# Attention inside an AdaLN block: value operands packed into one stationary tile, row sums of the exponentials on GpSimd, O kept for 1024 queries

## The chip, the cores and the metric

One core of one Trainium2 chip runs the whole program. The metric is the device time in microseconds. Five engines work beside each other, each through its own instructions in order, and wait for each other on semaphores: TensorE (PE), VectorE (DVE), ScalarE (ACT), GpSimd (POOL) and SyncE (SP, which only issues transfers here).

## The reference

All tensors are float32; x is 2 x 2048 x 256.

```
mod = (silu(c) @ wmod).reshape(2, 6, 1, 256)         # sa, ca, ga, sb, cb, gb
h = layernorm(x) * (1 + ca) + sa
x = x + ga * token_statistics_attention(h)           # the front of the kernel
h = layernorm(x) * (1 + cb) + sb
x = x + gb * ffn(h)

def ffn(X):                                          # 4 heads of 64
    nx = rmsnorm(X, g1)
    Q  = (nx @ Wq.T) in 4 heads;  Kc = nx @ Wkc.T;  Vc = nx @ Wvc.T     # K and V shared by the heads
    scores = einsum("bhsd,btd->bhst", Q, Kc) / 8
    X = X + (softmax(scores) @ Vc, heads side by side) @ Wo.T
    ... router over 8 experts, top 2, swiglu experts plus a shared one
```

## The kernel before

The program has three stages. The **front** (to about 233 us of the profile) makes the first residual and the first K, V and Q. The **loop** (about 235 to 1113 us) is the softmax attention of the second half. The **tail** runs 110 expert tiles and combines them.

The loop has 256 steps, numbered gs. A step belongs to one pair of batch and head, bh = gs // 32 (bh 0 to 3 are batch 0). In a bh, steps 0 to 15 take the first 1024 queries (qc = 0) and steps 16 to 31 the second 1024 (qc = 1), each against one block kc of 128 keys. Float32 products are made from fp32r parts: a high part, and a low part that is the value less its high part. One step is:

- `qk(gs)` on PE, 4 matmuls of 512 columns: scores, keys on the partitions, into banks 0 and 1, or 2 and 3.
- `exp(gs)` on ACT: `PT` = exp of the scores (L770), then `PH`, its rounded high part (L775). PT has 2 buffers, PH and PL have 3.
- `low(gs)`: `PL` = PT - PH (L1189 on DVE; every fourth step, up to step 243, L1514 on POOL, by `by_pool`). PT, PH and PL all lie in SBUF.
- `av(gs, n)` on PE, for each half n of 512 queries, 3 matmuls: VH x PH, VL x PH, VH x PL (L1749 to L1751), summed over the 16 key blocks in banks 4 and 5. VH carries a 65th column of ones and VL one of zeros, so that row 64 of the result is the sum of the exponentials.
- after the 16th key block, `o_out` copies 65 x 512 to `O` on ACT; `O` holds all 2048 queries of a bh.

PE runs, for each gs: `qk(gs + 1)`, jobs, `av(gs - 1, 0)`, jobs, `av(gs - 1, 1)`, jobs. DVE runs `low(gs)` and then the jobs of the step. The jobs are spread over the steps by `loop_order`, at positions 0 to 96 of a bh, three to a step. They are: `max_mm` (one matmul of 512 columns on PE, then a maximum over it on DVE, L1159; 64 for each bh, for the softmax shift), `proj` (O times Wo on PE, L1713, then DVE takes the reciprocal of column 256, L1176, and adds to X2, L1180; 16 for each bh, run during the next bh), and in some bh the making of the next Q (`q_mm`, `q_hi`: two ACT copies and two POOL copies of 64x512, L1507; `q_lo`: two DVE subtractions of 64x512, L1153), of K and V of batch 1 (`nx_scale`, `k_mm`, `v_mm`), the router (`rl_scale`, `choose`, `place`) and `scatter`. Every job with a result in PSUM takes bank 6 or 7 in turn (`Banks`): PE waits until the job two before has been read.

The wait of `exp` on the step two before stands in three lines:

```
            if gs >= 2:
                low_done(w, gs - 2)
            act.activation(PT[:, gs % 2, :], PS[:, bk:bk + 2, :].rearrange("p a n -> p (a n)"), ACT.Exp,
```

`after_last` makes each POOL instruction wait for the POOL instruction before it. The tail begins with 16 `proj` of bh 7, nine jobs a tile.

## Time and profile before

| | |
|---|---|
| median of 3 runs | 1458.81 us (1456.15 to 1462.72) |
| the profiled execution | 1461.01 us |
| its span, first to last instruction | 1459.0 us |
| mean granted TensorE clock | 0.967 of full speed |
| the loop in it | about 240 to 1113 us |
| busy over the span | PE 1307.4, DVE 1079.0, ACT 893.1, POOL 385.4 us |

A busy time is the union of an engine's instructions; those of PE overlap each other in the record, so that PE's share overstates its work: a matmul of 512 columns is recorded with some 395 ns and the next one starts 0.23 us after it. An instruction that is held up after its start is recorded longer, not as idle.

### The profile page before, as it was taken

To read this page: it belongs to the slowest core of one execution; us is meant where nothing else is said; L and a number is where in the kernel's file an instruction comes from. 1 tells how busy PE (TensorE), PEld (TensorE's weight loads), DVE (VectorE), ACT (ScalarE), POOL (GpSimd) and SP (SyncE) were. 2 spreads that over 40 slices of the span, in tenths; PEclk is the share of its full clock that TensorE was granted. 3 is DMA by queue.
4 is the path that set the end of the run, shared out by engine and by line. 5 is a ranking of instruction groups with operands and counts; after the bars stand their busy time and mean duration, and the time that the engine had idled before them with its cause. 6 is when DMAs were issued, how large, how long until landed. Compare 5 with 4: busy or idle time off the path is not lost.

```text
span 1459.0 us, 19334 instructions
## 1 busy us (share of the span) xinstructions
PE 1307.4 (90%) x6008; PEld 920.7 (63%) x6008; DVE 1079.0 (74%) x2143; ACT 893.1 (61%) x1450; POOL 385.4 (26%) x282
## 2 busy tenths in 40 slices
...
GB/s 196 1 1 44 15 58 208 81 1 1 1 1 1 1 1 1 1 1 1 1 1 1 1 1 44 1 0 1 22 51 65 104 93 117 195 148 165 191 115 149
DMA packets 56418, 75.82 MB, mean 52 GB/s; under 512 B 8383, under 2 KB 48063, under 8 KB 56064
## 3 DMA queue, kind: packets, MB, share of 16 engines
...
## 4 chain that ended last, share of the span: by engine, by line
PE 63%; DVE 19%; issue 5%; ACT 5%; POOL 5%; DMA 1%; ACTq 1%; POOLq 0%; DVEq 0%; SPq 0%
PE PS L1802 8%; PE PS L1700 6%; PE PS L1749 6%; PE PS L1732 6%; PE PS L1751 6%; PE PS L1735 6%; PE PS L1750 6%; DVE mx L1159 5%; PE PS L1828 4%; DVE PL L1189 4%; PE PS L1713 3%; POOL y L1534 2%; PE PS L1686 2%; POOL xbuf L1522 2%; PE PS L1786 1%
## 5 line engine op out<-in xcount | busy, mean ns | idle before, releaser
L1159 DVE TENSOR_REDUCE mx<-PS 128x1 f32<-128x512 f32 x512 | 344.1, 686 | 100.6 <-PE PS L1700 98.5
L770 ACT ACTIVATE PT<-PS 128x1024 f32<-128x1024 f32 x256 | 262.8, 1027 | 231.8 <-PE PS L1735 221.8
L1514 POOL TENSOR_TENSOR PL<-PT,PH 128x1024 fp32r<-128x1024 f32 x61 | 146.2, 2396 | 541.8 <-ACT PH L775 530.1
L775 ACT ACTIVATE PH<-PT 128x1024 fp32r<-128x1024 f32 x256 | 271.2, 1060 | 8.1
L1189 DVE TENSOR_TENSOR PL<-PT,PH 128x1024 fp32r<-128x1024 f32 x195 | 238.9, 1225 | 44.4 <-ACT PH L775 43.8
L1749 PE MATMUL PS<-PH,VH 128*65 128x512 f32 x512 | 219.6, 429 | 8.6 <-DVE PL L1189 8.6
L1751 PE MATMUL PS<-PL,VH 128*65 128x512 f32 x512 | 202.9, 396 | 0.0
L1750 PE MATMUL PS<-PH,VL 128*65 128x512 f32 x512 | 202.3, 395 | 0.0
L1700 PE MATMUL PS<-KA,Q 128*128 128x512 f32 x384 | 161.1, 432 | 16.9 <-DVE mx L1159 12.1
L1732 PE MATMUL PS<-Q,KA 128*128 128x512 f32 x384 | 128.0, 415 | 2.5 <-POOL KB L1491 2.5
L1735 PE MATMUL PS<-Q,KB 65*128 65x512 f32 x384 | 122.6, 401 | 0.0
L1700 PEld LDWEIGHTS PS<-KA,Q 128*128 128x128 f32 x384 | 73.5, 192 | 65.7 <-DVE mx L1159 35.4
L1751 PEld LDWEIGHTS PS<-PL,VH 128*65 128x65 f32 x512 | 69.7, 136 | 49.6 <-issue 1.0
L1750 PEld LDWEIGHTS PS<-PH,VL 128*65 128x65 f32 x512 | 70.2, 137 | 47.9 <-issue 4.6
L1522 POOL DMA_INDIRECT xbuf<-nxT,slot x64 | 64.0, 1000 | 134.7 <-DVE nxT L1347 117.4
L1749 PEld LDWEIGHTS PS<-PH,VH 128*65 128x65 f32 x512 | 70.2, 137 | 41.3 <-issue 13.6
L1713 PE MATMUL PS<-woa,O 65*128 65x257 f32 x256 | 80.8, 402 | 12.0 <-DVE mx L1159 8.6
L1534 POOL DMA_INDIRECT y<-ybuf,slot x64 | 62.1, 970 | 107.8 <-DVE X L1401 71.2
L1369 DVE TENSOR_TENSOR xl<-PS,xh 128x256 fp32r<-128x256 f32 x110 | 46.3, 421 | 56.4 <-ACT xh L857 56.1
L1735 PEld LDWEIGHTS PS<-Q,KB 65*128 65x128 f32 x384 | 73.7, 192 | 17.5
L1732 PEld LDWEIGHTS PS<-Q,KA 128*128 128x128 f32 x384 | 71.9, 191 | 19.9 <-issue 3.4
L864 ACT ACTIVATE sg<-PS 128x256 f32<-128x256 f32 x110 | 42.4, 385 | 59.9 <-PE PS L1802 59.7
...
## 6 DMA issues: line engine op xcount, KB each, us to landing
...
```

Source lines behind the costliest of these rows:

```text
L770: act.activation(PT[:, gs % 2, :], PS[:, bk:bk + 2, :].rearrange("p a n -> p (a n)"), ACT.Exp, scale=0.125).then_inc(sem("pt"), 1)
L775: act.activation(PH[:, gs % 3, :], PT[:, gs % 2, :], ACT.Copy).then_inc(sem("pt_h"), 1)
L1159: dve.tensor_reduce(mx[:, half, i, c:c + 1], PS[:, k, :], AX, ALU.max).then_inc(sem("dve_out"), 1)
L1189: dve.tensor_tensor(PL[:, gs % 3, :], PT[:, gs % 2, :], phf[:, gs % 3, :], ALU.subtract).then_inc(sem("pl_v"), 1)
L1514: pool.tensor_tensor(PL[:, gs % 3, :], PT[:, gs % 2, :], phf[:, gs % 3, :], ALU.subtract).then_inc(sem("pl_g"), 1)
L1700: pe.matmul(PS[:, k, :], QA[bh % 3][:, q0:q0 + P], KA[b][:, c * 512:c * 512 + 512], start=True, stop=True).then_inc(sem("pe_use"), 1)
L1713: pe.matmul(PS[:, k, 0:257], O[0:65, i * P:i * P + P], woa[0:65, bh % 4, :], start=True, stop=True).then_inc(sem("pe_use"), 1)
L1732: pe.matmul(PS[:, bk + n, :], KA[b][:, kc * P:kc * P + P], QA[qs][:, q0:q0 + 512], start=True, stop=False)
L1735: mm = pe.matmul(PS[:, bk + n, :], KB[b][0:65, kc * P:kc * P + P], QB[qs][0:65, q0:q0 + 512], start=False, stop=True)
L1749: pe.matmul(PS[0:65, 4 + n, :], VH[:, t, :], PH[:, r, c], start=(kc == 0), stop=False)
L1750: pe.matmul(PS[0:65, 4 + n, :], VL[:, t, :], PH[:, r, c], start=False, stop=False)
L1751: pe.matmul(PS[0:65, 4 + n, :], VH[:, t, :], PL[:, r, c], start=False, stop=(kc == 15)).then_inc(sem("av"), 1)
```

## The change

Four things. (1) VH and VL become one tile `V` of 128 columns, 64 high and 64 low: PH is multiplied once by all 128 columns, PL by the 64 high ones, 4 value matmuls a step in place of 6. Rows 64 to 127 of the result hold the part of VL; `proj` multiplies all 128 rows of O by Wo, written twice one under the other. (2) The ones column is gone. POOL keeps a running sum over the key blocks, `Z`, one 128x1024 instruction for each step (`total`: a copy for kc = 0, else Z = Z + PT), and `z_mm` multiplies Z by a column of ones on PE, once for every 1024 queries: 8 plain float32 matmuls of one column; DVE takes one reciprocal for 8 proj. (3) All 256 `low` are on DVE, PL has 2 buffers in place of 3, and `exp(gs)` waits for `low(gs - 2)` and `total(gs - 2)`. (4) O holds 1024 queries. `proj` of the first 1024 queries runs in the same bh (positions 53 to 92), those of the second in the next (5 to 46), so the tail keeps 8 `proj` and not 16.

```diff
-POOL_EVERY = 4
@@ loop_order
+        todo += [(50, ("z_mm", bh, 0))] + spread(proj_jobs(bh, 0), 53, 92)
         if bh > 0:
-            m, e = (30, 60) if bh == 4 else (49, 92)
-            todo += spread(proj_jobs(bh - 1)[:8], 4, m) + spread(proj_jobs(bh - 1)[8:], m + 1, e)
+            todo += [(3, ("z_mm", bh - 1, 1))] + spread(proj_jobs(bh - 1, 1), 5, 46)
@@ tail_order
-    last = [x for j, p in enumerate(proj_jobs(7)) for x in (p, norm[j])] + [norm[NT]]
+    last = [("z_mm", 7, 1)] + [x for j, p in enumerate(proj_jobs(7, 1)) for x in (norm[j], p)] + norm[8:]
@@ tiles
-    VH = sb("VH", [P, NB * NT, 65], F32R, c=c3)
-    VL = sb("VL", [P, NB * NT, 65], F32R, c=c3)
+    V = sb("V", [P, NB * NT, 2, 64], F32R, c=c3)
-    PL = sb("PL", [P, 3, 1024], F32R, c=c3)
-    O = sb("O", [65, S], c=c3)
-    woa = sb("woa", [65, 4, 257], c=c3)
+    PL = sb("PL", [P, 2, 1024], F32R, c=c3)
+    Z = sb("Z", [P, 2, 1024], c=c3)
+    O = sb("O", [P, 1024], c=c3)
+    woa = sb("woa", [P, 4, D], c=c3)
@@ ACT, exp
             if gs >= 2:
-                low_done(w, gs - 2)
+                w.wait_ge(sem("pl"), gs - 1)
+                w.wait_ge(sem("z"), gs - 1)
@@ DVE
+        def z_mm(bh, qc):
+            ...
+            dve.reciprocal(rz[:, qc, :], PS[:, k, 0:8]).then_inc(sem("dve_out"), 1)
@@ DVE, proj
-            mark(dve.reciprocal(rz[:, s, :], PS[:, k, 256:257]))
@@ DVE, low
-            if gs >= 3:
-                w.wait_ge(sem("av"), 2 * (gs - 2))
-            dve.tensor_tensor(PL[:, gs % 3, :], PT[:, gs % 2, :], phf[:, gs % 3, :], ALU.subtract).then_inc(sem("pl_v"), 1)
+            if gs >= 2:
+                w.wait_ge(sem("av"), 2 * (gs - 1))
+            dve.tensor_tensor(PL[:, gs % 2, :], PT[:, gs % 2, :], phf[:, gs % 3, :], ALU.subtract).then_inc(sem("pl"), 1)
@@ DVE loop
-            if not by_pool(gs):
-                low(gs)
+            low(gs)
@@ POOL
+        def total(gs):
+
+            g, kc = divmod(gs, 16)
+            w.wait_ge(sem("pt"), gs + 1)
+            if kc == 0:
+                ...
+                pool.tensor_copy(Z[:, g % 2, :], PT[:, gs % 2, :]).then_inc(sem("z"), 1)
+            else:
+                after_last("z")
+                pool.tensor_tensor(Z[:, g % 2, :], Z[:, g % 2, :], PT[:, gs % 2, :], ALU.add).then_inc(sem("z"), 1)
@@ POOL loop
-            if by_pool(gs):
-                low(gs)
+            total(gs)
@@ PE
+        def z_mm(bh, qc):
+            w.wait_ge(sem("ones"), 1)
+            w.wait_ge(sem("z"), 16 * (2 * bh + qc + 1))
+            k = bank("z_mm", bh, qc, 0)
+            for i in range(8):
+                mm = pe.matmul(PS[:, k, i:i + 1], Z[:, qc, i * P:i * P + P], ones[:, :], start=True, stop=True)
+            mm.then_inc(sem("pe_use"), 1)
@@ PE, av
-            pe.matmul(PS[0:65, 4 + n, :], VH[:, t, :], PH[:, r, c], start=(kc == 0), stop=False)
-            pe.matmul(PS[0:65, 4 + n, :], VL[:, t, :], PH[:, r, c], start=False, stop=False)
-            pe.matmul(PS[0:65, 4 + n, :], VH[:, t, :], PL[:, r, c], start=False, stop=(kc == 15)).then_inc(sem("av"), 1)
+            if kc < 15:
+                pe.matmul(PS[:, 4 + n, :], V[:, t, :, :].rearrange("p a d -> p (a d)"), PH[:, gs % 3, c], start=(kc == 0),
+                          stop=False)
+                pe.matmul(PS[0:64, 4 + n, :], V[:, t, 0, :], PL[:, gs % 2, c], start=False, stop=False).then_inc(sem("av"), 1)
+            else:
+                ...
```

What the change does to the order of POOL's instructions is seen from the last step of bh 0 on. Before, POOL stands there with the copies of `q_hi` (L1507) and one low part (L1514) for every fourth step; a number behind x counts repeated instructions.

```order
58 L1514 TENSOR_TENSOR PL<-PT,PH 128x1024
59 L1507 COPY Q<-Q 64x512
60 L1507 COPY QA<-QA 64x512
61 L1514 TENSOR_TENSOR PL<-PT,PH 128x1024 x13
```

After the change the same copies (now L1499) stand between the running sums (L1514) of every step; L1511 is the copy that begins a new sum.

```order
67 L1514 TENSOR_TENSOR Z<-Z,PT 128x1024 x4
68 L1499 COPY Q<-Q 64x512
69 L1499 COPY QA<-QA 64x512
70 L1514 TENSOR_TENSOR Z<-Z,PT 128x1024 x3
71 L1499 COPY Q<-Q 64x512
72 L1499 COPY QA<-QA 64x512
73 L1514 TENSOR_TENSOR Z<-Z,PT 128x1024 x4
74 L1511 COPY Z<-PT 128x1024
75 L1514 TENSOR_TENSOR Z<-Z,PT 128x1024 x15
```

POOL went from one 128x1024 instruction in four steps to one in each. The second place is the end of bh 7, where `scatter` issues its indirect transfers from POOL's queue. Before, the last low part of POOL lies ahead of all of them.

```order
69 L1514 TENSOR_TENSOR PL<-PT,PH 128x1024 x18
70 L1522 DMA xbuf<-nxT,slot 4992x256 x64
71 L1534 DMA y<-ybuf,slot 128x256 x40
```

After the change they alternate with the running sums, two or four transfers to a sum.

```order
103 L1514 TENSOR_TENSOR Z<-Z,PT 128x1024
104 L1522 DMA xbuf<-nxT,slot 4992x256 x4
105 L1514 TENSOR_TENSOR Z<-Z,PT 128x1024
106 L1522 DMA xbuf<-nxT,slot 4992x256 x2
107 L1514 TENSOR_TENSOR Z<-Z,PT 128x1024
108 L1522 DMA xbuf<-nxT,slot 4992x256 x4
```

Thirty-two of the transfers now have sums between them, and `exp` waits for these sums. The third place is DVE's stream in the middle of the loop. Before, steps whose low part is POOL's have no L1189, so that DVE's jobs of two steps follow each other.

```order
643 L1189 TENSOR_TENSOR PL<-PT,PH 128x1024
644 L1159 TENSOR_REDUCE mx<-PS 128x1 x2
645 L1176 RECIPROCAL rz<-PS 128x1
646 L1180 SCALAR_TENSOR_TENSOR X2<-PS,rz,X2 128x256
647 L1159 TENSOR_REDUCE mx<-PS 128x1 x2
648 L1176 RECIPROCAL rz<-PS 128x1
649 L1180 SCALAR_TENSOR_TENSOR X2<-PS,rz,X2 128x256
650 L1159 TENSOR_REDUCE mx<-PS 128x1
651 L1189 TENSOR_TENSOR PL<-PT,PH 128x1024
```

After, a low part (L1182) stands in every step, with two or three maxima (L1146) and at times a proj (L1173) behind it.

```order
659 L1182 TENSOR_TENSOR PL<-PT,PH 128x1024
660 L1146 TENSOR_REDUCE mx<-PS 128x1 x2
661 L1182 TENSOR_TENSOR PL<-PT,PH 128x1024
662 L1146 TENSOR_REDUCE mx<-PS 128x1 x3
663 L1182 TENSOR_TENSOR PL<-PT,PH 128x1024
664 L1146 TENSOR_REDUCE mx<-PS 128x1 x2
665 L1182 TENSOR_TENSOR PL<-PT,PH 128x1024
666 L1146 TENSOR_REDUCE mx<-PS 128x1
667 L1164 RECIPROCAL rz<-PS 128x8
```

The step-wise alternation of a low part and its jobs is now the same in all steps, and the reciprocal stands once for eight proj.

## Rows read from the trace of the kernel before

**Rows 1.** The page: busy time of each engine over the span.
```profile
PE 1307.4 (90%) x6008; PEld 920.7 (63%) x6008; DVE 1079.0 (74%) x2143; ACT 893.1 (61%) x1450; POOL 385.4 (26%) x282
```

**Rows 2.** Windows, the loop by bh: us, then busy us (instructions) per engine, clock.
```profile
240.00:331.00 91.00, 90.40 (x385) 61.56 (x384) 72.63 (x96) 67.18 (x67) 19.19 (x8) 1.00 0.27 91
...
558.00:678.00 120.00, 115.45 (x503) 78.26 (x501) 89.10 (x137) 77.19 (x85) 26.56 (x16) 0.99 0.00 1
...
1010.00:1113.00 103.00, 90.93 (x384) 60.04 (x383) 77.59 (x153) 66.72 (x70) 42.20 (x34) 0.98 0.13 44
sum 873.00, PE 834.36 PEld 557.81 DVE 667.73 ACT 590.55 POOL 202.41; mean PE 104.29 PEld 69.73 DVE 83.47 ACT 73.82 POOL 25.30
```

**Rows 3.** The page: costliest groups, busy us, mean ns, idle before and releaser.
```profile
L1159 DVE TENSOR_REDUCE mx<-PS 128x1 f32<-128x512 f32 x512 | 344.1, 686 | 100.6 <-PE PS L1700 98.5
L770 ACT ACTIVATE PT<-PS 128x1024 f32<-128x1024 f32 x256 | 262.8, 1027 | 231.8 <-PE PS L1735 221.8
L775 ACT ACTIVATE PH<-PT 128x1024 fp32r<-128x1024 f32 x256 | 271.2, 1060 | 8.1
```

**Rows 4.** Timeline, 602 to 605 us, PE and PEld: start, us, instruction.
```profile
602.38 0.40 PE L1751 MATMUL PS<-PL,VH 128*65 128x512 f32 x1
602.38 0.19 PEld L1700 LDWEIGHTS PS<-KA,Q 128*128 128x128 f32 x1
602.61 0.39 PE L1700 MATMUL PS<-KA,Q 128*128 128x512 f32 x1
```

**Rows 5.** One line's instructions, L1514 and L1189: ns min/median/max.
```profile
L1514 POOL TENSOR_TENSOR PL<-PT,PH x61: 2340/2393/2499, 245.2 to 1069.8; 128x1024 fp32r<-128x1024 f32 x61
...
L1189 DVE TENSOR_TENSOR PL<-PT,PH x195: 1210/1217/1503, 237.3 to 1111.1; 128x1024 fp32r<-128x1024 f32 x195
```

**Rows 6.** Timeline, 336 to 344 us: DVE and POOL about a `q_hi` and `q_lo`.
```profile
336.05 0.61 POOL L1507 CAST QA<-QA 64x512 fp32r<-64x512 f32 x1 [9.62 <-ACT QA L761]
...
336.30 1.44 DVE L1189 TENSOR_TENSOR PL<-PT,PH 128x1024 fp32r<-128x1024 f32 x1
...
336.81 1.40 POOL L1507 CAST Q<-Q 64x512 fp32r<-64x512 f32 x1 [0.16 <-POOL QA L1507]
...
339.52 2.50 POOL L1514 TENSOR_TENSOR PL<-PT,PH 128x1024 fp32r<-128x1024 f32 x1 [1.31 <-ACT PH L775]
...
339.80 2.77 DVE L1153 TENSOR_TENSOR Q<-qst,Q 64x512 fp32r<-64x512 f32 x1
```

**Rows 7.** One line's instructions, L1153, L1507 and L1159: ns min/median/max.
```profile
L1153 DVE TENSOR_TENSOR Q<-qst,Q x24: 671/687/2769, 201.0 to 833.3; 64x512 fp32r<-64x512 f32 x24
...
L1507 POOL CAST Q<-Q x24: 604/612/1457, 201.1 to 831.3; 64x512 fp32r<-64x512 f32 x24
...
L1159 DVE TENSOR_REDUCE mx<-PS x512: 627/690/694, 203.1 to 1051.2; 128x1 f32<-128x512 f32 x171
```

**Rows 8.** Groups by form: proj, its reciprocal, `nx_scale` and PE's small float32 matmuls.
```profile
L1180 DVE SCALAR_TENSOR_TENSOR X<-PS,rz,X 128x256 f32<-128x256 f32 x128 | 61.9, 484 | 4.5
...
L1176 DVE RECIPROCAL rz<-PS 128x1 f32<-128x1 f32 x128 | 20.7, 162 | 26.7 <-PE PS L1713 26.3
...
L1133 DVE TENSOR_SCALAR nx<-X,rs 128x256 f32<-128x256 f32 x32 | 17.2, 541 | 0.1
```

**Rows 9.** Timeline, 385 to 389 us: an `nx_scale` beside a low part on POOL.
```profile
385.53 2.41 POOL L1514 TENSOR_TENSOR PL<-PT,PH 128x1024 fp32r<-128x1024 f32 x1 [5.76 <-ACT PH L775]
...
386.39 1.71 DVE L1133 TENSOR_SCALAR nx<-X,rs 128x256 f32<-128x256 f32 x1
```

**Rows 10.** Timeline, PE, 843 us: four records of two 8-column float32 matmuls.
```profile
843.39 0.51 PE L1766 MATMUL PS<-wr,xT 128*128 128x8 f32 x4
```

**Rows 11.** Timeline, POOL in `scatter` of batch 0, 1074 to 1079 us.
```profile
1075.80 1.11 POOL L1522 DMA_INDIRECT xbuf<-nxT,slot  x1 [0.30 <-issue]
...
1077.22 0.96 POOL L1522 DMA_INDIRECT xbuf<-nxT,slot  x1 [0.30 <-issue]
...
1078.49 1.17 POOL L1522 DMA_INDIRECT xbuf<-nxT,slot  x1 [0.30 <-issue]
```

More of the change, by code:

```diff
@@ L127, in q_jobs, with proj_jobs @@
     return [(n, b, pair, c) for c in range(4) for n in ("q_mm", "q_hi", "q_lo")]
-def proj_jobs(bh):
-    return [("proj", bh, i) for i in range(NT)]
+def proj_jobs(bh, qc):
+    return [("proj", bh, 8 * qc + i) for i in range(8)]
 def norm_jobs(b):
@@ L231, in tail_order @@
     return {s: flat(v) for s, v in order.items()}
-def by_pool(gs):
-    return gs % POOL_EVERY == POOL_EVERY - 1 and gs < 7 * NSTEP + 20
-def lows(gs, pool):
-    return sum(by_pool(g) == pool for g in range(gs + 1))
 class Once:
@@ L346, in _build @@
     mT = sb("mT", [8, 2, P], F32R, c=c3)
-    rz = sb("rz", [P, 2, 1], c=c3)
+    rz = sb("rz", [P, 2, 8], c=c3)
+    ones = sb("ones", [P, 1], c=c3)
     wk = sb("wk", [P, 2, P], c=c3)
@@ L466, in attention_done @@
         w.wait_ge(sem("o"), 32)
[L467 to L468 removed]
+        w.wait_ge(sem("pl"), NGS)
+        w.wait_ge(sem("z"), NGS)
         w.wait_ge(sem("av"), 2 * NGS)
@@ L620, in _ @@
         front_done(w)
-        sp.dma_start(woa[:, :, :], I["woA"]).then_inc(sem("d_woa"), 16)
+        for a in (0, 64):
+            sp.dma_start(woa[a:a + 64, :, :], I["woA"][0:64, :, 0:D]).then_inc(sem("d_woa"), 16)
         w.wait_ge(sem("zero"), 1)
@@ L781, in o_out @@
                 return
-            q0 = qc * 1024 + n * 512
             w.wait_ge(sem("av"), 2 * gs + n + 1)
-            if bh:
-                pe_of(w, ("proj", bh - 1, 8 * qc + 7, 0))
-            act.activation(O[:, q0:q0 + 512], PS[0:65, 4 + n, :], ACT.Copy).then_inc(sem("o"), 1)
+            if qc:
+                pe_of(w, ("proj", bh, 7, 0))
+            elif bh:
+                pe_of(w, ("proj", bh - 1, 15, 0))
+            act.activation(O[:, n * 512:n * 512 + 512], PS[:, 4 + n, :], ACT.Copy).then_inc(sem("o"), 1)
         def norm(b, i):
@@ L1170, in max_turn @@
             dve.tensor_copy(mT[:, half, :], PS[0:8, k, 0:P]).then_inc(sem("dve_out"), 1)
+        def z_mm(bh, qc):
+            k = banks.bank["z_mm", bh, qc, 0]
+            pe_of(w, ("z_mm", bh, qc, 0))
+            if bh:
+                out_of(w, ("proj", bh - 1, 8 * qc + 7, 0))
+            dve.reciprocal(rz[:, qc, :], PS[:, k, 0:8]).then_inc(sem("dve_out"), 1)
         def proj(bh, i):
-            b, s, k = bh // 4, i % 2, banks.bank["proj", bh, i, 0]
-            n = b * NT + i
+            b, k = bh // 4, banks.bank["proj", bh, i, 0]
+            n, qc = b * NT + i, i // 8
             pe_of(w, ("proj", bh, i, 0))
-            mark(dve.reciprocal(rz[:, s, :], PS[:, k, 256:257]))
-            w.wait_ge(own, made[0])
+            out_of(w, ("z_mm", bh, qc, 0))
             if bh % 4:
                 out_of(w, ("proj", bh - 1, i, 0))
-            dve.scalar_tensor_tensor(X2[:, n, :], PS[:, k, 0:256], rz[:, s, :], X2[:, n, :], ALU.mult,
+            dve.scalar_tensor_tensor(X2[:, n, :], PS[:, k, 0:256], rz[:, qc, i % 8:i % 8 + 1], X2[:, n, :], ALU.mult,
                                      ALU.add).then_inc(sem("dve_out"), 1)
@@ L1420, in _ @@
                 "rsqrt2": rsqrt2, "nx_scale": nx_scale, "k_mm": k_mm, "v_mm": v_mm, "q_lo": q_lo, "max_mm": max_mm,
-                "max_row": max_row, "max_turn": max_turn, "proj": proj, "norm_root": norm_root,
+                "max_row": max_row, "max_turn": max_turn, "z_mm": z_mm, "proj": proj, "norm_root": norm_root,
                 "rl_scale": rl_scale, "rl_mm": rl_mm, "choose": choose, "count": count, "place": place,
@@ L1709, in proj @@
             qc, n = divmod(i, 8)
-            w.wait_ge(sem("d_woa"), 16)
+            w.wait_ge(sem("d_woa"), 32)
+            q0 = n * P
             w.wait_ge(sem("o"), 4 * bh + 2 * qc + n // 4 + 1)
             k = bank("proj", bh, i, 0)
-            pe.matmul(PS[:, k, 0:257], O[0:65, i * P:i * P + P], woa[0:65, bh % 4, :], start=True,
+            pe.matmul(PS[:, k, 0:D], O[:, q0:q0 + P], woa[:, bh % 4, :], start=True,
                       stop=True).then_inc(sem("pe_use"), 1)
+        def z_mm(bh, qc):
[5 more added lines that the diff above has]
+            mm.then_inc(sem("pe_use"), 1)
         def qk(gs):
@@ L1748, in av @@
                 w.wait_ge(sem("o"), 4 * bh + 2 * qc + n - 1)
[L1749 to L1751 removed]
+            if kc < 15:
[3 more added lines that the diff above has]
+            else:
+                pe.matmul(PS[0:64, 4 + n, :], V[:, t, 0, :], PL[:, gs % 2, c], start=False, stop=False)
+                pe.matmul(PS[:, 4 + n, :], V[:, t, :, :].rearrange("p a d -> p (a d)"), PH[:, gs % 3, c], start=False,
+                          stop=True).then_inc(sem("av"), 1)
         def rl_turn(b, i):
```

39 lines of the change are left out of this document (14 added, 25 removed), and 2 rows, old and new, of the table READERS.

## The prediction, made before the changed kernel was run

> **What bounds the kernel now.** I read the busy times first, then the windows of the loop, then the costliest groups, and last the timeline where two engines touch the same memory. The page gives PE 90% and POOL 26% [rows 1]. PE's share is inflated by overlap: in the timeline matmuls of 512 columns start 0.23 us apart (602.38, 602.61) though each is recorded with 0.4 [rows 4]. Per step PE has 4 matmuls of qk, 6 of av and about 2 of max_mm, 12 x 0.23 = 2.8 us, and with proj and the Q, K, V jobs about 3.1. The loop takes 873 us for 256 steps, 3.41 each, with DVE busy 668 of them, 2.61 a step [rows 2]. So neither is full: DVE waits 98.5 us for the max matmuls behind PE's other work, and ACT waits 221.8 us for scores and is not the bound [rows 3]. PE and DVE alternate through two banks, PE the nearer to its limit. The bh that make Q (558 to 678: 120 us) are slower than bh 0 (91 us) [rows 2].
>
> The decisive view is a short stretch, 336 to 344 us [rows 6]. At 336.05 POOL copies 64x512 in 0.61 us. DVE's low part starts at 336.30 and takes 1.44, not the median 1.217 [rows 5]. POOL's next copy starts at 336.81 and takes 1.40, where the median is 0.612 [rows 7]: it ends at 338.21, 0.47 after the low part (337.74). At 339.52 POOL runs its own low part, 2.50 us; DVE's `q_lo`, started at 339.80, takes 2.77 for work of median 0.687 [rows 6, 7] and ends 0.55 after POOL's (342.57 against 342.02). So a DVE instruction with two inputs in SBUF and a POOL instruction that reads SBUF don't share: the later one waits until the other is through. Of 32 `q_lo` the worst took 2.769 us [rows 7]. Maxima, which read PSUM, never exceed 0.694 us in 512 [rows 7], though POOL was often at work. I read this as one resource which the new kernel asks for twice in every step.
>
> **The change, part by part.** *PE.* 512 matmuls fewer, 512 x 0.23 = 118 us of PE's time in the loop, 0.46 a step. A 128-column stationary load takes 0.19 us and lies under the matmul ahead (0.23) [rows 4], so the wider operand costs nothing; if it did not hide, 1,024 loads would show up as gaps. PE then has about 2.7 us a step.
>
> *DVE.* 61 more low parts of 1.22 = 74 us [rows 5], 128 reciprocals of 0.162 fewer = 21 us [rows 8], 16 new ones of about the same size, 3 us. Busy time in the loop goes from 668 to 724 us, 2.83 a step, still under 3.41.
>
> *POOL.* 240 sums and 16 copies of 128x1024. A 128x1024 instruction of two inputs takes a median of 2.393 us [rows 5]; the sum has the same shape and I take 2.35 to 2.40. The 61 low parts go. That is some 600 us on an engine that was idle for most of the loop. Taken alone it would be hidden: 2.4 under 3.4.
>
> *The pair.* Per step the shared resource now serves a low part and a sum. From rows 6 the hand-over costs nothing, it even overlaps a little: a waiting DVE instruction ends 0.55 after POOL where it needs 0.687 alone, 0.13 less; a waiting POOL copy ends 0.47 after DVE where it needs 0.612, also 0.14 less. So a low part behind a sum adds 1.22 - 0.14 = 1.08, a sum behind a low part 2.36 - 0.14 = 2.22, together **3.30 us a step**. The sum starts when `PT` is written, the low part can start only 1.06 later, after `PH` [rows 3], so the sum comes first and the low part waits: from its end (t) the next sum runs to t + 2.22 and the next low part to t + 3.30. In this rhythm ACT keeps up (its exp needs the low part two steps before), and DVE's other jobs lie under the sum if they are shorter than 2.2 us. With 0.686 a maximum and 0.484 a proj [rows 3, 8], 38 of the 256 steps have more than that (three maxima and a proj make 2.54); they cost their jobs plus 1.22, by my count over the list of jobs 18 us more. **256 x 3.30 + 18 = 862 us**, against 873 before: what PE gives up is used up here.
>
> The Trainium skill, SBUF — State Buffer, section "SBUF: two separate sides", says that the pair of ports which VectorE and GpSimd share is locked for the whole instruction of whoever starts first, and the other blocks fully, with no sharing. The trace agrees with the blocking. Taken to the letter the rule leaves no overlap at the hand-over, which would make 3.58 of the 3.30; that is rival 2 below, and the sum here goes by the rows.
>
> *Lost turns.* The rhythm breaks when another DVE instruction of this kind stands between two low parts. It waits for the sum to end, then POOL, whose next operand is ready in steps with few jobs, starts the next sum before DVE comes to its low part: one more sum, 2.2 us, on DVE's path. Three kinds in the loop:
> - `q_lo`: 12 pairs in the loop (bh 1, 3, 5). Each of the two waits for a sum: 2.22 + 0.55, 2.25 + 0.55, then 1.22 of low part: 6.8 in place of 3.30, plus POOL's two copies, 1.2, and half a us of getting back: 5.2 x 12 = 62 us. Lower bound: only their own time on the resource, 12 x 2 x (0.69 + 0.61) = 31 us.
> - `nx_scale`, `rl_scale`: 32. One took 1.71 us beside POOL's low part, from 386.39 to 388.10, 0.16 after POOL's end at 387.94 [rows 9]; with the overlap of 0.14 its own work is some 0.3. The price lies between 0.3 and 2.4 + 0.3 each; in about half of the steps POOL's next operand is late (three or more bank jobs hold PE back before the next qk), so 1.4 each: 45 us.
> - `choose` and `place` in bh 7: 44 jobs over 14 steps, mostly short DVE instructions on SBUF. At most two sums can pass per low part, as the next exp waits for it. I take 5.5 us a step, halfway between 4.5 and 6.5: 14 x 2.2 = 31 us.
>
> *`scatter` behind the sums.* POOL issues 32 indirect transfers in the last 11 steps, each 1.0 to 1.2 us and 0.3 of issue [rows 11], 3 a step = 3.9 us. Before nothing waited for POOL there. Now the sum (2.35) is queued among them and `exp` waits for it: 6.3 us a step and 3.0 more than 3.30: 33 us. Behind `exp` stand qk and av, everything. bh 7 took 103 us [rows 2].
>
> *`z_mm`.* 8 plain float32 matmuls of one column. Two such of 8 columns are four records starting over 0.51 us [rows 10], about 0.11 a record: 16 records, 1.8 us. At position 50 it is the last job before the next low part and adds about 1.3 us to a step, 8 times: 10 us; at position 3 it is covered by PE's slack. Copies in place of sums in 16 steps give back some 6 us.
>
> *O and proj.* ACT's copies are as many, proj needs the same matmuls. 8 proj leave the tail: 8 x 0.48 [rows 8] = -4 us. The new waits of O on proj of the other half are met some two steps earlier; front and the expert tiles don't change.
>
> **Sum.** Loop: 862 + 62 + 45 + 31 + 33 + 10 - 6 = 1037, that is +164. With the tail, +160. The profiled execution took 1461.0 us with 2.0 outside its span, 2 us over the median of 1458.8: 1461 + 160 = 1621, on the median's basis **1619**; I give 1620.
>
> **The rivals.**
> 1. *The forecast's own case*: turns taken at 3.30, some lost. Low end, where turns are never lost: 862 + 31 (Q) + 10 (scales) + 10 (routing) + 20 (scatter) + 6 (z_mm) - 4 = 935, which is +62: 1520. High end: 77 steps have just two bank jobs. In them, once POOL's sum has got ahead of the low part, it stays ahead: exp 1.1 after the low part, then the sum, then the low part, 1.1 + 2.36 + 1.08 = 4.54. 77 x 1.3 = 100 more: 1720. Chance 0.70.
> 2. *Full serial turns*: no overlap, 1.22 + 2.36 = 3.58 a step. 0.28 x 256 = 72 us more than the forecast: 1692. Against it, the two ends of 0.47 and 0.55 in rows 6. Chance 0.10. It is what the page above says to the letter.
> 3. *The sums don't hold DVE up* (faster). For it: the long cases in rows 6 and 7 are few, and the low part's median beside all of POOL's work is 1.217 [rows 5]. Against it: a low part hardly ever ran beside one of POOL's, since the program gave each step to one of them. If it holds, DVE sets the pace: 724 busy, and of the 205 us that it idled in the loop about half, 100, now that PE has slack: 824, which is -49; less 4 and plus 10 for z_mm: 1418. The point that decides is the mean low part: 0.16 us more on each of 256 eats the 41 us, so it must stay under 1.38. PE's own time, 873 - 118 + 29 = 784 us of loop, would be the floor at about 1370. Chance 0.11.
> 4. *The floor alone*: 3.30 holds, the bh with Q get back what POOL's low parts had cost them, and lost turns and scatter are small: 1440 to 1475. Chance 0.05.
> 5. *Locked out all through*: the sum is ahead of the low part nearly always, 4.54 x 256 = 1162, and with the other terms about 1830. Against it: steps with three maxima delay the next qk until DVE has read the first, so POOL's operand comes after DVE's and the order is restored. Chance 0.04.
>
> A clock that falls because PE idles more would add to any of them. In the loop the granted clock was 0.98 to 1.00, also at 1010 to 1113 with PE busy 91 of 103 us [rows 2]; I count nothing.
>
> **How the numbers follow.** 1620 is the sum of case 1. Its own bounds are 1520 and 1720; case 2 lies inside. I reach to 1490 and 1730, since the prices of the lost turns are counted on few rows and the idle steps of bh 0 may bring some of it back: 0.78 to 0.8 of the chance. About 0.5%, 7 us, is what a measurement of this kernel can tell from no change. Slower: cases 1, 2, 5 and part of 4: 0.86. Same: 0.03. Faster: 0.11.
>
> **What would show it.** In the profile after, the low part on DVE with a mean of 2 us or more and not 1.22, with a maximum near 3.5; POOL's sums between 2.35 and 3.6, POOL busy over 60% of the loop; the maxima unchanged at 0.69. A loop of 1,000 us or more, bh 7 the longest of all. PE with visible gaps before the first value matmul, released by the low part. Wrong on the mechanism if the mean low part is 1.3 or less; wrong on the lost turns if the `q_lo` stay near 0.7 or if bh 0, which has none of these jobs, is as slow per step as bh 5; wrong on scatter if the last 11 steps take under 5 us each.

## The result: 17% slower

The changed kernel took 1710.8 us (median of 4; 1706.6 to 1714.4) against 1460.8 us (median of 4): a ratio of 1.171, 95% interval 1.165 to 1.176. The profiled execution has a span of 1712.5 us. From the first exp to the last, the loop went from 872 us (235.2 to 1107.2) to 1125 us (237.0 to 1361.9); front and tail stayed within 2 us. The whole difference of 250 us lies in the loop.

The page of the changed kernel, busy times and the slices of the TensorE clock, to be held against [rows 1]:

```profile
PE 1348.1 (79%) x5752; PEld 966.4 (56%) x5752; DVE 1333.6 (78%) x2092; ACT 892.1 (52%) x1450; POOL 896.8 (52%) x476
...
PEclk9897879888989988989998888898988579999998
```

PE has 256 fewer records (512 value matmuls gone, 256 of `z_mm` new), yet its busy time is larger: its matmuls are recorded longer, at a lower clock. DVE's busy time grew by 255 us, though its instructions became 51 fewer. The costliest groups say where, in answer to [rows 3]:

```profile
L1514 POOL TENSOR_TENSOR Z<-Z,PT 128x1024 f32<-128x1024 f32 x240 | 640.0, 2667 | 282.9 <-ACT PT L756 268.7
L1182 DVE TENSOR_TENSOR PL<-PT,PH 128x1024 fp32r<-128x1024 f32 x256 | 457.1, 1786 | 51.0 <-ACT PH L761 49.4
L756 ACT ACTIVATE PT<-PS 128x1024 f32<-128x1024 f32 x256 | 262.5, 1025 | 418.3 <-PE PS L1741 323.9
L1146 DVE TENSOR_REDUCE mx<-PS 128x1 f32<-128x512 f32 x512 | 339.4, 683 | 74.9 <-PE PS L1697 74.3
```

The low part went from 1.22 to a mean of 1.79 us, the sum takes 2.67 us where the shortest takes 2.34, the maxima stay at 0.68. Windows of the changed kernel for bh 0, 3, 4 and 7 (as [rows 2]: us, busy per engine, clock):

```profile
235.00:353.00 118.00, 94.78 (x350) 65.82 (x350) 103.67 (x113) 67.40 (x66) 85.47 (x32) 0.90 0.28 92
...
637.00:794.00 157.00, 123.28 (x466) 86.80 (x466) 122.08 (x130) 77.10 (x84) 89.58 (x40) 0.86 0.00 1
794.00:916.00 122.00, 99.47 (x387) 70.32 (x388) 106.20 (x121) 77.94 (x103) 84.40 (x32) 0.92 0.00 1
...
1206.00:1359.00 153.00, 107.63 (x373) 73.35 (x373) 114.99 (x149) 68.92 (x73) 102.15 (x57) 0.79 0.08 29
```

Every bh is slower, bh 7 by most (102 to 153 us, from its first exp to the last); the clock granted to TensorE is 0.79 to 0.92 where it was 0.98 to 1.00. The mechanism is seen in an ordinary stretch of bh 0, the timeline of DVE and POOL from 302 to 309 us:

```profile
304.28 5.69 POOL L1514 TENSOR_TENSOR Z<-Z,PT 128x1024 f32<-128x1024 f32 x2 [1.95 <-ACT PT L756]
305.33 2.43 DVE L1182 TENSOR_TENSOR PL<-PT,PH 128x1024 fp32r<-128x1024 f32 x1 [0.26 <-ACT PH L761]
307.68 1.28 DVE L1146 TENSOR_REDUCE mx<-PS 128x1 f32<-128x512 f32 x2
```

and the timeline of all engines from 307 to 316 us, which splits the second of these two sums off:

```profile
306.82 3.15 POOL L1514 TENSOR_TENSOR Z<-Z,PT 128x1024 f32<-128x1024 f32 x1
...
308.41 0.79 PE L1711 MATMUL PS<-woa,O 128*128 128x256 f32 x2 [2.03 <-DVE mx L1146]
...
309.43 0.63 PE L1759 MATMUL PS<-PL,V 128*64 128x512 f32 x1
...
309.85 0.63 PE L1697 MATMUL PS<-KA,Q 128*128 128x512 f32 x1
...
312.60 0.39 PE L1759 MATMUL PS<-PL,V 128*64 128x512 f32 x1
...
312.83 0.40 PE L1757 MATMUL PS<-PH,V 128*128 128x512 f32 x1
```

The first sum ends at about 306.67 (0.15 before the next starts), the low part that was started under it at 307.76 (305.33 + 2.43), 1.09 later; the second sum, started at 306.82, ends at 309.97, 2.21 after the low part. These are the 1.08 and 2.22 of the prediction, and they hold throughout the trace: of 134 low parts that start under a sum, 130 end 1.05 to 1.12 us after it. But this is not every low part: 121 of the 256 take under 1.3 us and are not held up. In bh 0 25 of 32 are held up, in bh 3 only 14 and in bh 7 only 9. PE then waits 2.03 us for a maximum behind the low part, and afterwards its matmuls start 0.42 us apart (309.43, 309.85) and not 0.23 (312.60, 312.83): the lower of its two clock levels, 1.2 GHz in place of 2.4 (the profile's granted clock is 0.62 of full speed from 308.4 to 310.4 us, and 1.00 from 306.0 to 308.4).

### The profile page after: what moved, and what is told of

It is laid out like the page before. It is cut to its first block, busy times and chain, and to the rows that moved or that the text cites. A ratio compares the mean times of both kernels' runs of the same rounds, so it can differ in the third digit from the quotient of the medians.

```text
span 1712.5 us, 19244 instructions
## 1 busy us (share of the span) xinstructions
PE 1348.1 (79%) x5752; PEld 966.4 (56%) x5752; DVE 1333.6 (78%) x2092; ACT 892.1 (52%) x1450; POOL 896.8 (52%) x476
## 4 chain that ended last, share of the span: by engine, by line
PE 38%; DVE 38%; issue 9%; ACT 6%; POOL 5%; DMA 2%; ACTq 1%; POOLq 0%; SPq 0%; DVEq 0%
DVE PL L1182 16%; DVE mx L1146 9%; PE PS L1814 7%; PE PS L1697 4%; PE PS L1840 4%; PE PS L1738 3%; PE PS L1741 3%; PE PS L1711 2%; PE PS L1757 2%; PE PS L1759 2%; PE PS L1683 2%; DVE Q L1140 2%; POOL xbuf L1522 2%; ACT PT L756 2%; POOL y L1534 1%
## 5 line engine op out<-in xcount | busy, mean ns | idle before, releaser
L1514 POOL TENSOR_TENSOR Z<-Z,PT 128x1024 f32<-128x1024 f32 x240 | 640.0, 2667 | 282.9 <-ACT PT L756 268.7
L1182 DVE TENSOR_TENSOR PL<-PT,PH 128x1024 fp32r<-128x1024 f32 x256 | 457.1, 1786 | 51.0 <-ACT PH L761 49.4
L1146 DVE TENSOR_REDUCE mx<-PS 128x1 f32<-128x512 f32 x512 | 339.4, 683 | 74.9 <-PE PS L1697 74.3
L1757 PE MATMUL PS<-PH,V 128*128 128x512 f32 x480 | 226.5, 472 | 23.4 <-DVE PL L1182 23.0
L1759 PE MATMUL PS<-PL,V 128*64 128x512 f32 x480 | 205.9, 429 | 0.0
L1757 PEld LDWEIGHTS PS<-PH,V 128*128 128x128 f32 x480 | 101.4, 211 | 61.9 <-issue 36.3
L1711 PE MATMUL PS<-woa,O 128*128 128x256 f32 x256 | 89.3, 437 | 41.8 <-DVE mx L1146 39.6
L1711 PEld LDWEIGHTS PS<-woa,O 128*128 128x128 f32 x256 | 50.7, 213 | 71.0 <-DVE mx L1146 55.0
L1697 PE MATMUL PS<-KA,QA 128*128 128x512 f32 x128 | 56.8, 445 | 36.8 <-DVE mx L1146 30.0
L1759 PEld LDWEIGHTS PS<-PL,V 128*64 128x64 f32 x480 | 71.7, 149 | 24.6 <-issue 3.3
L1173 DVE SCALAR_TENSOR_TENSOR X<-PS,rz,X 128x256 f32<-128x256 f32 x128 | 60.8, 476 | 26.3 <-PE PS L1711 26.0
```

Source lines behind the costliest of these rows:

```text
L1146: dve.tensor_reduce(mx[:, half, i, c:c + 1], PS[:, k, :], AX, ALU.max).then_inc(sem("dve_out"), 1)
L1182: dve.tensor_tensor(PL[:, gs % 2, :], PT[:, gs % 2, :], phf[:, gs % 3, :], ALU.subtract).then_inc(sem("pl"), 1)
L1514: pool.tensor_tensor(Z[:, g % 2, :], Z[:, g % 2, :], PT[:, gs % 2, :], ALU.add).then_inc(sem("z"), 1)
L1697: pe.matmul(PS[:, k, :], QA[bh % 3][:, q0:q0 + P], KA[b][:, c * 512:c * 512 + 512], start=True, stop=True).then_inc(sem("pe_use"), 1)
L1711: pe.matmul(PS[:, k, 0:D], O[:, q0:q0 + P], woa[:, bh % 4, :], start=True, stop=True).then_inc(sem("pe_use"), 1)
L1757: pe.matmul(PS[:, 4 + n, :], V[:, t, :, :].rearrange("p a d -> p (a d)"), PH[:, gs % 3, c], start=(kc == 0), stop=False)
```

## The experiments

Each kernel was timed in turn with the kernel before on its chip, and the ratio is to that kernel. A ratio's 95% interval is some 0.5% wide to each side, so a difference of two times below is known to some 10 us.

**1. Short sums.** All order and waits as changed; the sums touch 8 columns.

```diff
-                pool.tensor_copy(Z[:, g % 2, :], PT[:, gs % 2, :]).then_inc(sem("z"), 1)
+                pool.memset(Z[:, g % 2, :], 1.0).then_inc(sem("z"), 1)
...
-                pool.tensor_tensor(Z[:, g % 2, :], Z[:, g % 2, :], PT[:, gs % 2, :], ALU.add).then_inc(sem("z"), 1)
+                pool.tensor_tensor(Z[:, g % 2, 0:8], Z[:, g % 2, 0:8], PT[:, gs % 2, 0:8], ALU.add).then_inc(sem("z"), 1)
```

> The changed kernel, but each of GpSimd's running sums adds 8 of 1024 columns only and the first of each 16 is a memset to one (most of the sum of the exponentials is left out); order, waits and z_mm stay. Theory 1 (sums and low parts exclude each other): the mean low part falls from 1.786 to 1.22-1.25 us, the sums' 640 us go, and scatter no longer waits behind long sums; 1430 to 1480 us. Theory 2 (the time goes to z_mm, the clock, the second PL buffer and the new order of the jobs): stays above 1600.

Measured: 1464.9 us, ratio 1.003 (1.001 to 1.005). The low part, one line's instructions (ns min/median/max), and the window of the loop with short sums:

```profile
L1182 DVE TENSOR_TENSOR PL<-PT,PH x256: 1179/1217/1231, 239.5 to 1116.9; 128x1024 fp32r<-128x1024 f32 x128
```

```profile
240.00:1114.00 874.00, 788.37 (x3269) 554.26 (x3267) 710.45 (x1045) 587.49 (x654) 138.84 (x308) 0.97 0.05 18
```

No low part is longer than 1.231 us, where the longest of the changed kernel took 3.631. The length of the sums is 246 of the 250 us, and the clock is back at 0.97. It is not a gain either: with 118 us less of matmuls and no low part held up, the kernel is where it was.

**2. GpSimd as busy, but reading nothing.** Three memsets for each sum.

```diff
-                after_last("z")
-                pool.tensor_tensor(Z[:, g % 2, :], Z[:, g % 2, :], PT[:, gs % 2, :], ALU.add).then_inc(sem("z"), 1)
+                for n in range(2):
+                    after_last("z1")
+                    pool.memset(Z[:, g % 2, :], 1.0).then_inc(sem("z1"), 1)
+                after_last("z")
+                pool.memset(Z[:, g % 2, 0:256], 1.0).then_inc(sem("z"), 1)
```

> The changed kernel, but each running sum on GpSimd is replaced by three memsets of the same tile (1024, 1024 and 256 columns, about 2.3 us together with their gaps), which read nothing from SBUF; the sum of the exponentials is left out. GpSimd is as busy, and exp waits for it as before. Theory 1 (what excludes is the reading of SBUF by both): the low parts take 1.22 to 1.3 us, near the run with light sums plus the scatter that waits behind them, 1460 to 1530. Rival (GpSimd's latency in the wait of exp, or any activity of it): within 3% of 1711.

Measured: 1502.8 us, ratio 1.028 (1.023 to 1.033). Two groups of its page:

```profile
L1515 POOL MEMSET Z<- 128x1024 f32 x480 | 458.1, 954 | 205.6 <-ACT PT L756 179.4
...
L1182 DVE TENSOR_TENSOR PL<-PT,PH 128x1024 fp32r<-128x1024 f32 x256 | 314.0, 1227 | 70.9 <-ACT PH L761 68.1
```

The three memsets last as long as a sum that nothing holds up (2 x 0.95 + 0.31 and their gaps, 2.33 us in all, against 2.34 for the shortest sum), exp waits for them by the same semaphore, and the low part takes 1.227. The Trainium skill, SBUF — State Buffer, section "Who interferes with whom", says that a DVE instruction with two SBUF inputs contends with a GpSimd instruction that reads SBUF and not with one that only writes it; by that, the trace agrees (1.227 against 1.786 us). So 208 us of the change (1710.8 - 1502.8) go with the sums reading SBUF, and 38 (1502.8 - 1464.9) with GpSimd being busy at all. Of these 38, the loop has 31, and bh 7 with its scatter 17 (131 us from exp to exp, 114 with short sums).

**3. z_mm with one matmul.**

```diff
-            for i in range(8):
+            for i in range(8 if bh == 0 and qc == 0 else 1):
```

> The changed kernel with one matmul of one column in 15 of the 16 z_mm in place of 8 (the other seven column sums are left out). By the prediction's term z_mm costs 10 us in all: 1695 to 1705. Rival: a z_mm also drags TensorE's granted clock down for the matmuls behind it (in the profile the 16 records take 2.65 us and the next matmuls start 0.43 us apart), and costs 4 to 5 us each at the middle of each bh: 1630 to 1670.

Measured: 1698.9 us, ratio 1.163 (1.159 to 1.167): 12 us less than the changed kernel, where the prediction had 10. The intervals of the two ratios touch (1.165 to 1.176 there), but the steps in question agree: step 17 of bh 1 to 7, where the edit leaves seven matmuls out, takes 29.3 us in all against 42.6, or 1.9 less each. The dragging clock that the rival saw behind the 16 records (they take 2.65 us at 294.26) is contained in these numbers and not separated from the matmuls' own time; the rival's 41 us and more are excluded.

**4. Six value matmuls.** Part (1) undone, all else as changed.

```diff
-                pe.matmul(PS[:, 4 + n, :], V[:, t, :, :].rearrange("p a d -> p (a d)"), PH[:, gs % 3, c], start=(kc == 0),
-                          stop=False)
-                pe.matmul(PS[0:64, 4 + n, :], V[:, t, 0, :], PL[:, gs % 2, c], start=False, stop=False).then_inc(sem("av"), 1)
...
+            pe.matmul(PS[0:64, 4 + n, :], V[:, t, 0, :], PH[:, gs % 3, c], start=(kc == 0), stop=False)
+            pe.matmul(PS[0:64, 4 + n, :], V[:, t, 1, :], PH[:, gs % 3, c], start=False, stop=False)
+            pe.matmul(PS[0:64, 4 + n, :], V[:, t, 0, :], PL[:, gs % 2, c], start=False, stop=(kc == 15)).then_inc(sem("av"), 1)
```

> The changed kernel with part (1) undone: six value matmuls a step again (high times PH, low times PH, high times PL, 64 columns each), all else as changed. Theory 1: TensorE has slack, so 118 us of matmuls come back mostly in its gaps: 1710 to 1750. Rival, the clock: with more work TensorE is granted a higher clock (0.85-0.92 in the loop now) and the time falls below 1700. Rival, TensorE is the bound: up to 1825.

Measured: 1728.2 us, ratio 1.182 (1.178 to 1.186). The windows of the loop, of the changed kernel and of this one:

```profile
240.00:1362.00 1122.00, 871.97 (x3268) 600.45 (x3267) 929.70 (x1045) 588.70 (x655) 708.55 (x310) 0.88 0.04 14
```

```profile
240.00:1372.00 1132.00, 971.68 (x3777) 601.72 (x3776) 916.62 (x1044) 589.78 (x653) 698.49 (x309) 0.92 0.04 14
```

118 us of matmuls cost 17, of which the loop has 11: in the changed kernel most of TensorE's saving lies in slack. The clock is 0.92 with the extra work and 0.88 without; that may hide a part of the 118, and no run separates it.

**5. Short sums only where scatter is.** In the last 12 steps, 244 to 255.

```diff
-                pool.tensor_tensor(Z[:, g % 2, :], Z[:, g % 2, :], PT[:, gs % 2, :], ALU.add).then_inc(sem("z"), 1)
+                if gs < 7 * NSTEP + 20:
+                    pool.tensor_tensor(Z[:, g % 2, :], Z[:, g % 2, :], PT[:, gs % 2, :], ALU.add).then_inc(sem("z"), 1)
+                else:
+                    pool.tensor_tensor(Z[:, g % 2, 0:8], Z[:, g % 2, 0:8], PT[:, gs % 2, 0:8], ALU.add).then_inc(sem("z"), 1)
```

(The steps in question are those from 7 x 32 + 20 = 244 on; the expectation names 228 by mistake and 244 beside it.)

> The changed kernel, but in the last 12 steps of the loop (228 to 255, where scatter issues its transfers from GpSimd's queue: 244 on) the running sums add 8 of 1024 columns (the rest of these sums is left out). By the prediction scatter behind the sums costs 33 us: 1670 to 1685. Rival: the low parts and exp there wait for the transfers themselves, which stay in GpSimd's queue ahead of each sum, short or long (the run with light sums still has 4.7 us a step there): only the length of the sums goes, 12 to 20 us: 1690 to 1700.

Measured: 1689.3 us, ratio 1.157 (1.152 to 1.163): 21 us less; the last ten steps take 46.7 us where they took 65.1, so 18 us of it are found there. The result is at the rival's edge and off the forecast's: with short sums a pair of these steps still takes 9.4 us (5.82 and 3.54 between starts of exp), with full ones 13.0 (8.2 and 4.8), and 6.6 by the prediction's 3.30 floor. The timeline of the changed kernel there, 1310 to 1326 us, ACT, DVE and POOL:

```profile
1309.99 1.02 ACT L756 ACTIVATE PT<-PS 128x1024 f32<-128x1024 f32 x1 [7.23 <-POOL Z L1514]
1310.04 0.98 POOL L1522 DMA_INDIRECT xbuf<-nxT,slot  x1 [0.17 <-DVE nxT L1340]
...
1311.33 0.96 POOL L1522 DMA_INDIRECT xbuf<-nxT,slot  x1 [0.30 <-issue]
1312.14 3.63 DVE L1182 TENSOR_TENSOR PL<-PT,PH 128x1024 fp32r<-128x1024 f32 x1 [2.10 <-ACT PH L761]
1312.32 2.35 POOL L1514 TENSOR_TENSOR Z<-Z,PT 128x1024 f32<-128x1024 f32 x1
1314.79 1.02 ACT L756 ACTIVATE PT<-PS 128x1024 f32<-128x1024 f32 x1 [2.68 <-POOL Z L1514]
```

POOL issues two transfers, then the sum that exp has been waiting for; exp starts 0.12 after the sum ends (1314.67). The exp at 1309.99 had waited 7.23 us for the sum before. The transfers stand ahead of each sum whether it is long or short.

**6. Every fourth sum in full.** The short sums of experiment 1, but 1024 columns where gs % 4 is 3.

```diff
+                n = 1024 if gs % 4 == 3 else 8
+                pool.tensor_tensor(Z[:, g % 2, 0:n], Z[:, g % 2, 0:n], PT[:, gs % 2, 0:n], ALU.add).then_inc(sem("z"), 1)
```

> The run with light sums, but each fourth step (gs % 4 == 3) has the full sum of 1024 columns (three of four steps add 8 columns; the rest is left out). If each full sum costs its own share of the 246 us between light and full, 1.0 us: 60 sums, 1525. If a single sum can hide beside the maxima and only sums in a row cost (both wait for each other in turn): 1465 to 1490.

Measured: 1532.7 us, ratio 1.048 (1.042 to 1.053). 68 us for 60 sums, 1.13 each, against 246 for 240, 1.02 each. A sum pays this price by itself; it doesn't need a row of them.

**7. The packed operand alone.** From the kernel before: the 128 columns are 64 high, the ones, and 63 low ones; the row sums stay on TensorE. The low part of the last of 64 value columns is left out.

```diff
+    V = sb("V", [P, NB * NT, P], F32R, c=c3)
...
+            dve.tensor_tensor(V[:, n:n + 4, 65:128], PS[:, k, 0:256].rearrange("p (t d) -> p t d", d=64)[:, :, 0:63],
+                              vf[:, n:n + 4, 0:63], ALU.subtract).then_inc(sem("dve_out"), 1)
...
+            pe.matmul(PS[:, 4 + n, :], V[:, t, :], PH[:, r, c], start=(kc == 0), stop=False)
+            pe.matmul(PS[:, 4 + n, :], V[:, t, :], PL[:, r, c], start=False, stop=(kc == 15)).then_inc(sem("av"), 1)
```

> The kernel before with the value operand packed only: one stationary tile of 64 high columns, the column of ones and 63 low columns, used for PH and for PL, 4 value matmuls a step; row sums stay on TensorE, every fourth low part on GpSimd, order as before (the low part of the last of 64 value columns is left out). Theory 1 (TensorE's work was part of the pace, and only the sums spoiled the change): 1400 to 1440. Rival (VectorE and the two banks set the pace, as the run with light sums suggests, which is no faster than before with 118 us less of matmuls): 1450 to 1465.

Measured: 1415.9 us, ratio 0.970 (0.965 to 0.975). The window of its loop:

```profile
240.00:1064.00 824.00, 745.53 (x3004) 541.05 (x3003) 666.46 (x1070) 586.16 (x654) 196.05 (x114) 0.98 0.05 18
```

From first to last exp the loop takes 827 us, 45 less than before: of 118 us of matmuls 45 were part of the pace, and DVE's work is unchanged (666 us; 668 before). Packing was the good part of the change.

**8. O for 1024 queries on top of it.** Part (4), on the kernel of experiment 7.

```diff
+        todo += spread(proj_jobs(bh, 0), 53, 92)
+        if bh > 0:
+            todo += spread(proj_jobs(bh - 1, 1), 5, 46)
```

> The run before plus part (4) of the change: O for 1024 queries, proj of the first half in the same bh, 8 proj fewer in the tail, no z_mm. If the new places of proj are harmless: 4 to 8 us below the packed run. Rival: they crowd DVE's jobs (the last proj of a half now follows the maxima of a busy stretch, and the tail only gives back 4 us): 5 to 20 us above it.

Measured: 1420.7 us, ratio 0.973 (0.968 to 0.977), 5 us over experiment 7. The intervals overlap. In the traces the loop takes 838 us against 827, and the stretch behind the last exp 346 against 350: the tail gives back its 4 us and the loop loses more, as the rival had it.

The last four kernels were timed on another chip, on which the stretch behind the last exp took 375 to 377 us in each of them where it had been 345 to 355 in all runs so far, and the kernel before took 1491.1 us. They are compared by their ratios and by their loops; the first 17 steps of bh 0 take 53.6 us in the changed kernel and 53.6 in experiment 11, so single steps do agree across the chips.

**9. All low parts on DVE.** The kernel of experiment 7 with `POOL_EVERY = 10000`.

> The packed kernel (ones column, row sums on TensorE; the low part of the last value column left out) with all 256 low parts on DVE and none on GpSimd: part (3) of the change without the sums. If the 61 low parts of GpSimd are a help to DVE: 74 us more of DVE work, of which a half shows, 1440 to 1460. Rival: they cost as much as they save, since each takes 2.39 us in the chain of its step and blocks DVE's two-input work beside it: 1405 to 1425.

Measured: ratio 0.978 (0.973 to 0.982), the loop 844 us against 827. By its ratio it would take some 1427 us on the first chip, just outside the rival's range (1405 to 1425) and well below the first theory's: of 74 us more work on DVE, 17 show in the loop and 11 by the ratios, not a half. Of the 17, 9 lie in the last steps of bh 0 to 6 (43.0 us in all against 34.3).

**10. Every third low part on GpSimd.** `POOL_EVERY = 3`.

> The packed kernel with every third low part on GpSimd in place of every fourth (the low part of the last value column left out). If DVE's load sets the pace: 20 low parts fewer on it, 24 us of its work, 1400 to 1412. Rival: the longer chain of a step with GpSimd's low part costs more than that: 1418 to 1435.

Measured: ratio 0.979 (0.974 to 0.983), the loop 852 us. The rival is right that it is worse than every fourth: by 24 us of loop, in an execution 6 us above its median, and by 13 us by the ratios. That the longer chain of a step is the cause is argued and not shown.

**11 and 12. The last maxima of a bh earlier.** One edit, in the changed kernel and in that of experiment 7:

```diff
-            todo += spread(max_jobs(bh + 1, 0), 42, 88) + spread(later[:5], 90, 95.9)
+            todo += spread(max_jobs(bh + 1, 0), 42, 88) + spread(later[:5], 88, 92.5)
```

> The changed kernel, only with the first five maxima of the next half placed at positions 88 to 92.5 and not 90 to 95.9, so that none stands between the last step of a bh and the qk of the next. In its profile the last step of a bh takes 6.7 to 9.9 us, since three max matmuls stand ahead of the next qk and their maxima behind blocked low parts; the prediction priced it like any other step. If this is the missing term: 4 to 5 us in each of 7 places, 1675 to 1685. Rival: the same maxima cost the same wherever they stand: 1700 to 1712.

> The packed kernel with the same five maxima moved (the low part of the last value column left out). Its last steps take 4.2 to 4.8 us against 3.1 for a mean step: if they come down by 1 to 1.5 us in 7 places, 1405 to 1409; rival, no change: 1412 to 1420.

Measured for the changed kernel: ratio 1.147 (1.142 to 1.154) against 1.171, the loop 1094 us against 1125, 31 less; by the ratio that is 1674 us on the first chip, at the edge of its theory's 1675 to 1685. The last steps of bh 0 to 6 fell from 6.7 to 9.9 us to 2.6 to 5.1, but the steps ahead of them, which now have the maxima, grew: the last two steps together went from 86.0 to 62.7 us over the seven places, so 23 of the 31 are found there. The timeline of the changed kernel before the edit, 346 to 357 us, shows what stood there:

```profile
346.31 2.82 DVE L1182 TENSOR_TENSOR PL<-PT,PH 128x1024 fp32r<-128x1024 f32 x1
...
349.79 1.39 PE L1697 MATMUL PS<-KA,Q 128*128 128x512 f32 x2 [2.10 <-DVE mx L1146]
...
350.25 2.17 DVE L1182 TENSOR_TENSOR PL<-PT,PH 128x1024 fp32r<-128x1024 f32 x1
...
353.08 0.80 PE L1697 MATMUL PS<-KA,Q 128*128 128x512 f32 x1 [1.90 <-DVE mx L1146]
353.25 0.76 PEld L1738 LDWEIGHTS PS<-Q,KA 128*128 128x128 f32 x2
...
355.62 1.02 ACT L756 ACTIVATE PT<-PS 128x1024 f32<-128x1024 f32 x1 [7.62 <-PE PS L1741]
```

Three max matmuls stand ahead of the qk of the next bh; they wait for maxima, these stand behind two held-up low parts, and exp waits 7.62 us for qk.

Measured for the packed kernel: ratio 0.962 (0.958 to 0.967), the lowest of all kernels here; its loop takes 822 us against 827. By the ratio that is 1404 us on the first chip, by the loop some 1410; the interval overlaps that of experiment 7 (0.965 to 0.975), so its forecast of 1405 to 1409 is not settled against no change.

## Why the prediction was right, and 90 us short

The forecast was slower, 1620 us, with 1490 to 1730; 1710.8 came out. Slower at 0.86 was right, by the mechanism of its own case: sum and low part take turns. The result lies 19 us under the upper bound. That bound was made from 77 steps with two jobs at 4.54 us, not from what was missing, so that it holds the result is in part luck.

*The turns.* Shown. 1.09 and 2.21 us at 306 to 310 us against 1.08 and 2.22; the 30 steps of bh 0 other than 17 and 31 (which have z_mm and the maxima ahead of qk) take a mean of 3.36 us, by the starts of their exp, where the sum had 862 / 256 = 3.37. Many of them come as a short and a long one in turn, 2.3 and 4.4, so that the 3.36 is a mean of pairs. Experiment 1 shows that the sums' length is the cause, experiment 2 that five sixths of it (208 of 246 us) go with their reading SBUF, experiment 6 that each sum pays. Rival 2 (no overlap, 3.58) is out by the hand-over of 1.08 us; its 1692 us lay nearer to the result than the forecast's 1620, and the total alone would have spoken for it.

*The signs.* The mean low part was to be 2 us or more and is 1.786, since half of them are not held up; bh 7 was to be the longest and takes 153 us, behind bh 3 and 5 with 157 and 158. The others came: a longest low part of 3.63 us, GpSimd busy for 708.6 of 1122 us, maxima at 0.68, over 5 us a step at the end (65.1 for the last ten).

*The faster rival*, 1418, is out by its own sign: the mean low part is not under 1.38. Its price was wrong too. Experiments 1 and 2 are that case made real, the low parts at 1.217 and 1.227 us, and they took 1464.9 and 1502.8. In experiment 1 DVE idled 164 us in the loop (874 - 710), not 100. Its loop of 877 us can be put together from experiment 7's 827: O for 1024 queries 11 (experiment 8), 61 more low parts on DVE 17 (experiment 9), z_mm 12 (experiment 3, with full sums), and the transfers ahead of short sums 11 (the last ten steps take 45.3 us against 34.4), 878 in all. That leaves nothing to speak of for PL's 2 buffers in place of 3, which no run changes alone. The prediction's 724 us of work for DVE was a little off as well: 16 of the 128 reciprocals were in the tail and not in the loop, and 8 proj come into the loop; by the same rows that makes 731, and the trace with short sums has 710.

*The sum, term by term* (loop only; 1037 forecast, 1125 measured). Measured sizes are differences between starts of exp, less 3.30 a step:

| term | forecast | measured |
|---|---|---|
| z_mm | 10 | 12, give or take 10 (experiment 3), for seven of eight matmuls |
| scatter behind the sums | 33 | 32 (last 10 steps: 65.1 us); only 18 of it go with the sums' length |
| Q in bh 1, 3, 5 | 62 | 78 (first 13 steps: 68.0, 70.5, 68.4 us); 21 of it stand there with short sums too (49.2, 51.5, 49.1) |
| choose and place | 31 | 15 (14 steps: 61.1 us) |
| nx_scale, rl_scale | 45, 1.4 each | not measured by themselves; see below |
| maxima ahead of the next qk | not priced | 31 (experiment 11) |

Of the 88 us that are missing, 31 are the maxima. Q adds 16 and routing gives back 16: that they cancel is luck. For the rest, the starts of exp by bh (us; bh 7 to its last exp). The last line is what the length of the sums costs, known to some 5 us: experiment 5, which is the changed kernel up to step 243, differs from it by up to that much in single ones of bh 0 to 6.

| bh | 0 | 1 | 2 | 3 | 4 | 5 | 6 | 7 |
|---|---|---|---|---|---|---|---|---|
| before | 91 | 116 | 111 | 120 | 103 | 120 | 108 | 102 |
| short sums (experiment 1) | 94 | 112 | 114 | 117 | 104 | 115 | 108 | 114 |
| changed | 119 | 147 | 137 | 157 | 122 | 158 | 132 | 153 |
| changed less short sums | 25 | 35 | 23 | 40 | 17 | 43 | 25 | 40 |

The scales are not what is missing. Without steps 17 and 31, bh 2 and 6 (15 scales) take 4.1 and 4.0 us a step against 3.36 in bh 0, 42 us in all; but with short sums too they take 3.45 and 3.21 against 2.74, and 35 of the 42 stand there. The sums' length costs no more in these two (23 and 25 us) than in bh 0 (25), which has no scale, so that lost turns of the scales don't show. The step of the prediction that failed is the one that said 38 steps "cost their jobs plus 1.22" and all others 3.30, as if the turns took the place of whatever pace a step had. In a bh with more jobs the steps were slower already, and the length of the sums came on top of that, 17 to 25 us in bh 0, 2, 4 and 6, 35 to 43 where Q is made, 40 in bh 7. And it counted the jobs of a step and not their place: at the end of a bh they stand before qk, on PE's way to the next exp, and a held-up low part holds them too. How the 57 us beside the maxima divide among single jobs stays open.

*The clock.* "I count nothing" was wrong as a statement on the clock: 0.88 in the loop for 0.99, with a fall after such a wait as the 2.03 us before 308.41. What it costs in time stays open. It comes back to 0.97 in experiment 1 together with the turns, and no run here changes it alone; a part of the term-by-term sizes above may be the clock's.

*TensorE's saving.* The forecast said that it is used up by the turns, and that is nearly so: experiment 4 takes it back for 17 us. In the kernel before it is worth 45 (experiment 7).

*The q_lo check.* The prediction asked for `q_lo` beyond 0.7 us; the timeline of bh 1, 363 to 382 us, has the pair at 1.69 and 2.72 us (with short sums no `q_lo` takes over 0.99):

```profile
366.30 8.77 POOL L1514 TENSOR_TENSOR Z<-Z,PT 128x1024 f32<-128x1024 f32 x3
...
368.42 1.69 DVE L1140 TENSOR_TENSOR QB<-qst,QA 64x512 fp32r<-64x512 f32 x1
...
370.14 2.72 DVE L1140 TENSOR_TENSOR Q<-qst,Q 64x512 fp32r<-64x512 f32 x1
...
373.49 2.66 DVE L1182 TENSOR_TENSOR PL<-PT,PH 128x1024 fp32r<-128x1024 f32 x1
```

Three sums follow each other, each with a DVE instruction held under it.
